# A two-layer transformer block on one core: wave-stage products and rounding on GpSimd, another order at the seam, SiLU per half, deviations on VectorE

## The reference

```python
x = layernorm(x + L0_attn(x))   # a wave field
x = layernorm(x + L0_ffn(x))    # fp4 gate, up, down
x = layernorm(x + L1_attn(x))   # windowed attention
x = layernorm(x + L1_ffn(x))    # top-2 of 8 experts + shared expert
# L0_attn, per head: deposit = (elu(k)+1) * v
# kernel = exp(-alpha t) cos(omega t + phi), normalised
# convolved = causal convolution of deposit with kernel (by FFT)
# out = (elu(q)+1) * coupled(convolved) * sigmoid(gate) @ Wout.T + bout
# L0_ffn: each block of 16 values is scaled to 6, rounded to the
# grid 0, .5, 1, 1.5, 2, 3, 4, 6 and scaled back, weights too
# layernorm: (x - mean) / sqrt(var + 1e-5)
```

## Time and profile before

| | us |
|---|---|
| median of 3 runs (lowest to highest) | 1100.16 (1098.81 to 1102.42) |
| the profiled execution, whole | 1101.61 |
| its span from first to last instruction | 1099.7 |
| busy in it: PE, VectorE, ScalarE, GpSimd | 1032.2, 764.7, 489.6, 442.0 |
| mean granted TensorE clock in it | 0.977 of the upper level |

### The profile page before, as it was taken

The page is one execution under the profiler, slowest core; times in us unless marked ns, Lnnn a source line. Parts: engine busy times, 40 slices in busy tenths (PEclk is TensorE's granted clock), DMA queues, the critical chain, the costliest instruction groups (busy, mean ns, idle before and its releaser), DMA issues.

```text
span 1099.7 us, 19315 instructions
## 1 busy us (share of the span) xinstructions
PE 1032.2 (94%) x5960; PEld 901.9 (82%) x5961; DVE 764.7 (70%) x1290; ACT 489.6 (45%) x914; POOL 442.0 (40%) x445
## 2 busy tenths in 40 slices
PE   6898997799999999999999999989999999999994
PEld 5676776799999998999988787878888888888883
DVE  7988998899999987787878343333444444347886
ACT  6745755774344444666751222222322222233326
POOL 1000201555544446322100787975633200018886
PEclk9999998999999999999999999999999999999997
DMA  8100000010000000311250557464413111213335
GB/s 315 70 32 20 1 29 1 1 35 1 0 0 0 0 1 1 120 40 39 64 205 6 187 172 242 141 183 160 156 52 107 56 48 54 70 58 108 123 106 191
DMA packets 41350, 87.83 MB, mean 80 GB/s; under 512 B 5970, under 2 KB 27732, under 8 KB 39892
## 3 DMA queue, kind: packets, MB, share of 16 engines
q0 software_dynamic: 9696, 35.66, 10.5%
q1 hardware_dynamic: 20804, 39.20, 10.0%
q10 hardware_dynamic: 10800, 12.32, 3.6%
HBM read 57.80 MB, written 29.36 MB: 79 GB/s over the span
## 4 chain that ended last, share of the span: by engine, by line
PE 53%; DVE 19%; DVEq 10%; POOL 8%; issue 5%; ACT 4%; DMA 1%; ACTq 0%; POOLq 0%
PE PS L1857 14%; PE PS L1859 13%; PE PS L1858 13%; POOL gathered L1043 6%; PE PS L2260 3%; PE PS L2012 2%; DVEq L1433 2%; DVEq L1280 2%; POOL pause L1047 1%; DVEq L1447 1%; PE PS L2244 1%; DVE hx L1292 1%; PE PS L1910 1%; DVEq L1293 1%; DVE qinv L1283 1%
## 5 line engine op out<-in xcount | busy, mean ns | idle before, releaser
L1794 DVE TENSOR_TENSOR hb<-PS,gs 128x512 f32<-128x512 f32 x71 | 49.1, 692 | 154.0 <-ACT gs L784 143.4
L1043 POOL DMA_INDIRECT gathered<-expert_outputs,pos x64 | 66.7, 1043 | 139.5 <-DMA expert_outputs<-ye 127.2
L1857 PE MATMUL PS<-EWs,xeh 128*128 x284 | 119.8, 422 | 0.0
L784 ACT ACTIVATE gs<-PS 128x512 f32<-128x512 f32 x71 | 42.5, 598 | 162.3 <-PE PS L1859 154.0
L1859 PE MATMUL PS<-EWs,xel 128*128 x284 | 112.5, 396 | 0.0
L1858 PE MATMUL PS<-EWs,xeh 128*128 x284 | 111.8, 394 | 0.0
L1857 PE MATMUL PS<-WGh,bxh 128*128 128x352 f32 x256 | 88.0, 344 | 13.4 <-DVE hv L1427 10.5
L2012 PE MATMUL PS<-WD,htf 128*128 128x256 f32 x384 | 88.5, 380 | 1.6 <-ACT htf L573 1.5
L1857 PE MATMUL PS<-EWs,heh 128*128 x284 | 85.7, 302 | 3.9 <-issue 3.9
L789 ACT ACTIVATE heh<-PS 128x512 fp32r<-128x512 f32 x71 | 42.5, 598 | 104.4 <-PE PS L2260 86.9
L1798 DVE TENSOR_TENSOR hel<-PS,heh 128x512 fp32r<-128x512 f32 x71 | 49.1, 691 | 55.0 <-ACT heh L789 46.3
(11 more groups left out here) (387 smaller groups left out, 3013.5 us busy)
## 6 DMA issues: line engine op xcount, KB each, us to landing
raw_of<-experts POOLq DMA_DIRECT2D x6, 1536.0 KB
expert_outputs<-ye SPq DMA_DIRECT2D x71, 128.0 KB
xe<-tokens_by_expert ACTq DMA_DIRECT2D x65, 128.0 KB
xraw<-xT SPq DMA_DIRECT2D x8, 512.0 KB, 4.1
X<-x SPq DMA_DIRECT2D x1, 4096.0 KB, 13.3
tokens<-X SPq DMA_DIRECT2D x8, 512.0 KB, 3.1
y<-X SPq DMA_DIRECT2D x7, 512.0 KB
raw_of<-experts SPq DMA_DIRECT2D x2, 1536.0 KB, 9.5
```

Source lines behind the costliest of these rows:

```text
L784: act.activation(gs[:, h], PS[:, 2], ACT.Silu).then_inc(e_si, 1)
L1043: pool.indirect_dma_start(out=gathered[c][:, j, t], out_offset=None, in_=YS, in_offset=bass.IndirectOffsetOnAxis(ap=pos[:, j, 4 * c + t:4 ...
L1794: dve.tensor_tensor(hb[:, h], PS[:, 3], gs[:, h], ALU.mult).then_inc(e_hb, 1)
L1857: pe.matmul(out_, wh, vh, start=first, stop=False)
```

## The change

- `recurrences`: VectorE keeps F1 and the first half of F2; GpSimd makes the other half (`deposit_turned`) and F1 = S1·cosB (`field_turned`), 1024 elements. VectorE waits for `turned` before the second S2 scan and before Y.
- GpSimd also takes the two products Wv·cosB, the rounding of the output bias into two parts (obr, onr), and both `early_dequantised`. Its two input splits are cut into halves that alternate with the new products. In batch 0 `mix_scale` goes ahead of Y.
- VectorE's `to_grid` of the second weights follows `conv(2)`, ahead of the third batch; `weights_low(3)` goes ahead of `residual(3)`.
- ScalarE: features of batches 2 and 3 go ahead of moments and normalisation; `attention_normalise(1)`, the load of the SiLU table and that of `attention_normalise(2)` go earlier, the sizing of w_down later.
- w_down's scaling moves into `step(0)`, its grid step into `step(1)`; GpSimd's `inverse_deviation(2)` goes ahead of its dequantisation. TensorE transposes weight group 3 earlier, into PSUM bank 0 instead of 6 and without a wait for the low half before it, and groups 4 and 5 inside `step(2)`.
- Experts: `e_gu` counts each half; SiLU waits for the gate half, the product for both.
- End: the deviations of chunks 0 to 4 are made on VectorE by `inverse_roots(5)`, a bit-shift start and four Newton steps; GpSimd's root of chunks 0 to 3, which stood ahead of its last gather, is gone. ScalarE normalises chunks 0 to 4 inside the last shared step.

```diff
             features(2, 0)
             wave(1, 1)
+            features(2, 1)
             means(0)
-            features(2, 1)
             variances(0)
             early_size(1)
 
+            features(3, 0)
             attention_normalise(0)
-            features(3, 0)
             wave(2, 0)
+            features(3, 1)
             means(1)
-            features(3, 1)
             variances(1)
...
             x_size(0, 0)
+            attention_normalise(1)
...
+            def down_size():
+                act.wait_ge(q_scaled, 3)
+                act.activation(wq2[:], wq1[:], ACT.Abs, scale=MAGIC).then_inc(q_sized, 1)
+
             step(-1, 1)
-            attention_normalise(1)
-            act.wait_ge(q_scaled, 3)
-            act.activation(wq2[:], wq1[:], ACT.Abs, scale=MAGIC).then_inc(q_sized, 1)
             step(0, 0)
+            down_size()
             variances(2)
...
-                wait(act, e_gu, i - 1)
+                wait(act, e_gu, 2 * i - 2)
...
-                act.wait_ge(e_gu, i + 1)
+                act.wait_ge(e_gu, 2 * i + 1)
...
-            shared(7, chunks=((), (), ((0, 0, 4),), ((1, 0, 4),)))
-            for c in range(2, NCH - 1):
+            shared(7, chunks=(((0, 0, 4),), ((1, 0, 4),), ((2, 0, 4),), ((3, 0, 4), (4, 0, 4))))
+            for c in range(5, NCH - 1):
...
-            def split_low(c):
+            def split_low(c, k):
                 pool.wait_ge(x_hi, c + 1)
-                pool.tensor_tensor(xl[:, c % 2], xraw[:, c % 2], xh[:, c % 2].bitcast(F32), ALU.subtract).then_inc(x_lo, 1)
-
-            pool.wait_ge(scanned, 2)
-            split_low(5)
+                last_ = pool.tensor_tensor(xl[:, c % 2, k], xraw[:, c % 2, k], xh[:, c % 2, k].bitcast(F32), ALU.subtract)
+                if k == KD - 1:
+                    last_.then_inc(x_lo, 1)
+
+            def deposit_turned(b):
+                pool.wait_ge(scanned, 2 * b + 1)
+                pool.tensor_tensor(F2[:, 1], DEP[:, 1], sinA[:, 1], ALU.mult).then_inc(turned, 1)
+
+            def field_turned(b):
+                pool.wait_ge(scanned, 2 * b + 2)
+                pool.tensor_tensor(F1[:], S1[:], cosB[:], ALU.mult).then_inc(turned, 1)
+
+            def early_dequantised(g):
+                pool.tensor_tensor(we[g][:].rearrange("p (b e) -> p b e", e=BLK), we[g][:].rearrange("p (b e) -> p b e", e=BLK),
+                                   wes[:, g].unsqueeze(2).to_broadcast([P, 2 * FFP // BLK, BLK]), ALU.mult).then_inc(wq_b, 1)
+
+            deposit_turned(0)
+            field_turned(0)
+            for m in range(KD):
+                pool.wait_ge(act_s, 14 + m)
+                pool.tensor_tensor(Wv[:, 0, m, 0:CH], Wv[:, 0, m, 0:CH], cosB[:, m], ALU.mult).then_inc(kernel_set, 1)
+            pool.wait_ge(ld_wo, 32)
+            pool.tensor_tensor(onr[:], C[0:2, C_ONE:C_ONE + P], zrow[0:2, 0:P], ALU.add)
+            pool.tensor_tensor(obr[:, 1], ob[:], zrow[0:2, :], ALU.add)
...
+            pool.tensor_tensor(obr[0:1, 0], ob[0:1, :], zrow[0:1, :], ALU.add).then_inc(ob_rows, 1)
+            pool.wait_ge(dve_v, KD * 3 + 1)
+            split_low(5, 0)
+            deposit_turned(1)
+            split_low(5, 1)
+            field_turned(1)
+            pool.wait_ge(q_grid, 1)
+            pool.wait_ge(wave0, coupled(1) + 1)
+            early_dequantised(0)
+            pool.wait_ge(dve_v, KD * 5 + 1)
+            split_low(7, 0)
+            deposit_turned(2)
+            split_low(7, 1)
+            field_turned(2)
             inverse_deviation(0)
-            pool.wait_ge(scanned, 3)
-            split_low(7)
+            pool.wait_ge(q_grid, 2)
+            early_dequantised(1)
+            deposit_turned(3)
+            field_turned(3)
             inverse_deviation(1)
...
             step(0, 0)
+            inverse_deviation(B - 2)
             pool.wait_ge(q_grid, 3)
             dequantise(wrow[:], wq1[:], wsc[:], 2 * FFP, wq_b)
-            inverse_deviation(B - 2)
...
-            pool.wait_ge(d_mv, 4)
-            deviation4(0, 0, 4)
             gather(NCH - 1)
             pool.wait_ge(d_mv, 6)
-            deviation4(1, 4, 6)
+            deviation4(0, 5, 6)
...
-            def recurrences(tables=0):
+            def recurrences(b):
                 dve.tensor_tensor(F1[:], DEP[:], cosA[:], ALU.mult)
-                dve.tensor_tensor(F2[:], DEP[:], sinA[:], ALU.mult)
-                dve.drain()
+                dve.tensor_tensor(F2[:, 0], DEP[:, 0], sinA[:, 0], ALU.mult).then_inc(scanned, 1)
+                dve.drain()
+                if b == 0:
+                    dve.wait_ge(act_s, 2 * KD + 9)
                 for m in range(KD):
-                    dve.tensor_tensor_scan(S1[:, m], sm[:, 18, m:m + 1].to_broadcast([P, CH]), F1[:, m], 0.0, ALU.mult, ALU.add)
-                wait(dve, act_s, tables)
+                    scan = dve.tensor_tensor_scan(S1[:, m], sm[:, 18, m:m + 1].to_broadcast([P, CH]), F1[:, m], 0.0, ALU.mult, ALU.add)
+                scan.then_inc(scanned, 1)
                 for m in range(KD):
-                    scan = dve.tensor_tensor_scan(S2[:, m], sm[:, 18, m:m + 1].to_broadcast([P, CH]), F2[:, m], 0.0, ALU.mult, ALU.add)
-                    if m == 0:
-                        scan.then_inc(scanned, 1)
-
-            def rotate():
-                dve.drain()
-                dve.tensor_tensor(F1[:], S1[:], cosB[:], ALU.mult)
+                    if m == 1:
+                        dve.wait_ge(turned, 2 * b + 1)
+                    dve.tensor_tensor_scan(S2[:, m], sm[:, 18, m:m + 1].to_broadcast([P, CH]), F2[:, m], 0.0, ALU.mult, ALU.add)
+
+            def rotate(b):
+                dve.drain()
                 dve.tensor_tensor(F2[:], S2[:], sinB[:], ALU.mult)
-                dve.drain()
+                if b == 0:
+                    mix_scale()
+                dve.drain()
+                dve.wait_ge(turned, 2 * b + 2)
...
-            recurrences(tables=2 * KD + 7)
+            recurrences(0)
...
-            for m in range(KD):
-                dve.wait_ge(act_s, 14 + m)
-                dve.tensor_tensor(Wv[:, 0, m, 0:CH], Wv[:, 0, m, 0:CH], cosB[:, m], ALU.mult).then_inc(kernel_set, 1)
-            rotate()
+            rotate(0)
...
-            dve.wait_ge(ld_wo, 32)
-            dve.tensor_copy(onr[:], C[0:2, C_ONE:C_ONE + P])
...
             to_grid(we[0][:], wm[:], q_grid)
-            early_dequantised(0)
...
             half(2, 0, 1)
             conv(2)
+            dve.wait_ge(q_sized, 2)
+            to_grid(we[1][:], wm[:], q_grid)
...
             residual(2, 0, 2)
-            dve.wait_ge(q_sized, 2)
-            to_grid(we[1][:], wm[:], q_grid)
             weights_low(0)
             residual(2, 2, 4)
             wave_last_column(3)
...
-            early_dequantised(1)
             weights_low(1)
             x_to_grid(0, 0)
             weights_low(2)
+            weights_low(3)
             residual(3)
-            weights_low(3)
...
-                if weights:
+                if weights and u == 1:
...
+                if weights and u == 0:
+                    dve.wait_ge(ld_b2, 16)
+                    largest(wsc[:], wrow[:])
+                    scales(wsc[:], winv[:])
+                    over_scale(wq1[:], wrow[:], winv[:], q_scaled)
...
-            step(1, 1)
+            step(1, 1, weights=True)
...
+            def inverse_roots(end):
+                varied, root, spare = mv4[:, 0:end, :, 1], rstd4[:, 0:end], nmr4[:, 0:end]
+                dve.drain()
+                dve.tensor_scalar(varied, varied, EPS, None, ALU.add)
+                dve.drain()
+                dve.tensor_scalar(spare.bitcast(U32), varied.bitcast(U32), 1, None, ALU.logical_shift_right)
+                dve.drain()
+                dve.tensor_scalar(root.bitcast(U32), spare.bitcast(U32), -1.0, float(0x5F3759DF), ALU.mult, ALU.add)
+                for _ in range(4):
+                    dve.drain()
+                    dve.tensor_tensor(spare, root, root, ALU.mult)
+                    dve.drain()
+                    dve.scalar_tensor_tensor(spare, spare, -0.5, varied, ALU.mult, ALU.mult)
+                    dve.drain()
+                    dve.scalar_tensor_tensor(root, spare, 1.5, root, ALU.add, ALU.mult)
+                dve.drain()
+                dve.scalar_tensor_tensor(spare, mv4[:, 0:end, :, 0], -1.0, root, ALU.mult, ALU.mult).then_inc(d_rs, end)
...
+                        if d == 4:
+                            inverse_roots(5)
...
+                dve.wait_ge(e_gu, 2 * i + 2)
...
-            shared(6, (((4, 1), (4, 2)), ((4, 3),), ((), (5, 0)), ((5, 1), (5, 2))), ((3,), (), (), (4,)))
-            shared(7, (((), (5, 3)), ((6, 0), (6, 1)), ((6, 2), (6, 3)), ()), ((5,), (), (), (6,)))
+            shared(6, (((4, 1), (4, 2)), ((4, 3),), ((), (5, 0)), ((5, 1), (5, 2), (5, 3))), ((3,), (), (), (4,)))
             last = NCH - 1
-            gated(last, 0)
-            gated(last, 2)
```

(15 more changed lines are left out.)

39 lines of the change are left out of this document (14 added, 25 removed).

## The result

The changed kernel takes 1121.39 us (median of 4, 1119.67 to 1123.55) against 1100.53 before: ratio 1.0199, 95% interval 1.0184 to 1.0215, or 20.9 us more. Forecast were 1109 and a range up to 1114: the sign was right, the size less than half. The profiled execution took 1123.55 us with a span of 1121.6.

The account below looks back on a forecast made before the run. PE carries 53% of the chain of waits, VectorE 19%, nearly level in the wave stage. Wave 7.7, seam 2.0, experts −2.0 and end 1.2 sum to +8.9 us: 1110.5, or 1109 against the median; range 1089 to 1114.

Parts of the forecast that it names:

- behind it: Wave stage after the last Y: second dequantisation gone from VectorE (−1.7), earlier low halves and transposes 0 to 0.8; −1.9 us taken.
- the seam: Between wave stage and experts: −2.4 for hs freed, +2.8 dequantisation, +1.6 grid steps; +2.0 us, bounds −3 and +3.
- the end: Last shared steps: roots lengthen VectorE's chain, ScalarE no longer last; +1.2 us, bounds −1.3 and +2.7.
- up to the last Y: Wave stage until its last field: −11.0 work removed, +21.3 stalls, −4.2 waits, +3.5 grid step; +9.6 us.
- the experts: Expert stage: SiLU beside the up half lets hb start sooner where PE waits at its transposes; −2.0 us, bounds −6 and +0.5.
- The blocking rule: Shared SBUF port: at a boundary the waiting engine, VectorE or GpSimd, gets in; the other stands for its whole operation.
- the stalls: Wave stage up to the last Y: GpSimd's added work between VectorE's two-operand operations stops VectorE for 21.3 us together.
- ScalarE's late features: Wave stage: features moved ahead of means and normalisation remove VectorE's two waits of 2.1 us between 105 and 112; −4.2 us.
- Rivals 1 and 2: Rival 1: no blocking that matters, 1089 us, chance 0.20; rival 2: VectorE keeps the port through back-to-back operations, 1100.5, 0.22.
- rival 3: Wave stage: PE's new waits lower its mean clock to 0.91, matmuls 5.9 us longer; 1114 us, chance 0.08.
- The term of the roots: End of shared step 6: 16 small VectorE operations, 3.8 us, partly taken up by later waits; +2.5 on VectorE's chain.

Follow-up runs that it names:

- b_silu: The kernel before with only the experts' part of the change (e_gu counted per half, SiLU after the gate half): ratio 0.9985 to before.
- b_features: The kernel before with only ScalarE's new wave-stage order (features of batches 2 and 3 ahead of means and normalisation): ratio 0.9984 to before.
- b_silu_features: The kernel before with both SiLU per half and ScalarE's new order in the wave stage: ratio 0.9957 to before.
- b_best: The kernel before with SiLU per half, ScalarE's new wave-stage order and the first early dequantisation on GpSimd: ratio 0.9968 to before.

## Why the prediction was right or wrong

The direction was right, 8.9 us forecast against 20.9. In the spans of the first pair 13.0 us are missing from the forecast; the steps that failed are "behind it", where a gain was counted that did not come (3.0 of them), the seam, which had no term for the moved transposes (2.9), and the end, where the reach of the roots was mis-sized (4.2). The rest is 1.5 up to the last Y, 0.6 in the experts, and 0.8 between the last down product and the first expert product, where the code is the same and no cause is shown.

- **The blocking rule was right, both ways and in size.** Forecast up to the last Y were +9.6, measured +11.1 and +9.6, and the stalls add up to 21.6 us where I had 21.3. The half products cost about 1.08 and the field products 2.15 each, as 1.06 and 2.12 had it; Wv 2.1; the second dequantisation 2.6 where I had 2.8. Of ScalarE's late features 0.6 us of waiting is left in batch 2 of the first pair. The Trainium skill, "SBUF — State Buffer", section "Who interferes with whom", states the blocking, though not which engine gets in at the boundary of two VectorE operations; the traces agree, with 4.50 us for a pair of scans of 2.35, and with 2.45 unchanged for the additions that read PSUM. Rivals 1 and 2 fall: no scan pair escaped.
- **"Behind it ... I take −1.9" was wrong in sign.** Measured +1.1 and +2.1. VectorE shed the work as said, but PE had waited 5.87 us and paid 2.0 us in clock on the coupling behind. The stretch scatters by up to 3 us between single profiles, as said at the table; the changed order's mean of nine is 30.6 us, that of before's three 30.1, so that the gain did not come is surer than the size of the loss. The clock is rival 3's mechanism; the rival gave it 5 us for the whole stage.
- **The seam: +2.0 forecast, +4.9 and +5.1 measured.** The gain was there: VectorE's first hx scaling started at 206.4 instead of 199.5, 6.9 late where the first gate product was 12.2 late. The grid step (3.5) and the stretched bx (2.5) gave it back. What I did not price at all is the step that cost: transposes 4 and 5 inside step 2. I had the edit before me and no term for it, though it puts ScalarE's wait, with hs queued behind, into a step. Taking them out is worth 3.4 us of the seam in the profiles (about 5 in the time), and the seam is then 1.7 longer than before, near the +2.0 that I had for the terms I did price; that these were right one by one is not shown.
- **The experts: −2.0 forecast, −1.4 and −3.4 in the profiles, 1.6 alone in the time.** The size was right. The mechanism is not borne out: I counted the gain on PE's waits at hb's transposes, and these fall by only 0.5 us (b_silu) and 0.4 (5.7 to 5.3, first pair).
- **The end: +1.2 forecast, +5.4 and +5.5 measured (last two rows of the table).** The term of the roots was mis-sized in its reach, not its length: 3.8 us forecast, 4.4 measured. I let VectorE's later waits take up 1.3 and put the rest against the 1.3 us by which ScalarE ended after VectorE. But hb stands right behind the roots, and PE, for which I had no term there, waited and then ran at the lower clock; and on the slower chips a second cause set the same end, GpSimd's gathers without the root between them. The removal of that root I had noted as a relief of the queue only.
- The range ended at 1114, where each term's upper bound was taken as unlikely beside the others. The three terms missed, behind the last Y, at the seam and at the end, erred to the same side, by 3 to 4 us each. Two of them share a reason: a late VectorE also costs PE its clock, which the sum never priced.

## What to carry to other kernels

Moving work from VectorE to GpSimd can pay where VectorE reads PSUM or has a single SBUF operand meanwhile (2.37 us of GpSimd work beside four additions of 2.45, 2.82 beside a reduction); between operations with two it costs its whole GpSimd time, about twice what VectorE would have needed (2.15 against 1.14 us for 1024 elements). So release it by the semaphore whose successor reads PSUM, not by the earliest possible one. And look again after every reordering: GpSimd's old work can slide into a bad place, as the split did in b_features. In a pipeline written by hand every moved instruction needs a price, above all a wait with other work queued behind on the same engine; and small dependent operations count where another engine waits for the very next one (3.4 us of the first gap for twelve of them). Before a single profile's difference of 1 or 2 us is explained, compare profiles of kernels that are the same there.

## What was not expected of the hardware

- PE was held within groups of matmuls while GpSimd issued its last sixteen gathers without a break; with 5 us of pause ahead of the last eight the third gap fell from 9.4 to 4.5 us. It came on the chips on which before took 1098 to 1101 us, not where it took 1087.
- Behind a wait of 5.87 us PE's granted clock averaged 0.67 over 6 us, and eight matmuls took 2.0 us longer. Behind waits of 2.65 us the same eight took 3.69 us at 1.00 in b_features, but 5.38 at 0.72 in b_silu_features and in b_best.
- The same kernel before took 1087.1 us on one chip and 1100.5 on another; the experts' stage alone differs by 12 (371.0 and 359.3 us).
